# Causal masks of the score maxima: from four 64x128 tile products to four 64x64 tile products

## What is computed

```python
# layer 0
scores = einsum('bhqd,bhkd->bhqk', q, k) / sqrt(8)
causal = triu(ones((s, s), dtype=bool), 1)
scores = where(causal, -inf, scores)
attn_w = softmax(scores, axis=-1)
attn   = einsum('bhqk,bhkd->bhqd', attn_w, v)
```

## Time and profile before

| | |
|---|---|
| three runs | 1511.41, 1514.30, 1517.33 us (median 1514.3) |
| the profiled execution's own time | 1513.78 us |
| its span, first to last instruction | 1512.0 us |
| mean granted clock of PE, of full speed | 0.964 |
| busy share of the span | PE 90%, DVE 83%, ACT 71%, POOL 18% |
| L391 (mask of the maxima) | 1024 matmuls, 68.5 us busy, 222 ns mean |
| layer 0's max units | from 47.2 to 462 us |

### The profile page before, as it was taken

How to read it: one execution, slowest core, us unless ns; L and a number is a source line. 1 busy time by engine, 2 the same in 40 slices (tenths; PEclk the granted TensorE clock), 3 DMA queues, 4 the chain that set the end, 5 groups by cost and what they waited for, 6 DMA issues and landing times.

```text
span 1512.0 us, 31977 instructions
## 1 busy us (share of the span) xinstructions
PE 1366.1 (90%) x13016; PEld 565.2 (37%) x13016; DVE 1251.6 (83%) x1715; ACT 1079.6 (71%) x1239; POOL 278.4 (18%) x624
## 2 busy tenths in 40 slices
PE   6699999999998768888679999999999999999886
PEld 3334434444443235456323332332333333323455
DVE  8988888888884386985899999999999999997043
ACT  6167777777777567763358888888888888888652
POOL 5022313222222151431100000000000000001252
PEclk9689999999999989999889999999999999999998
DMA  5510111101000000021110000000000000000001
GB/s 179 169 44 24 39 31 31 40 24 46 24 4 2 1 1 0 1 81 67 42 64 24 23 24 23 24 21 14 16 23 24 23 23 24 3 3 3 1 15 42
DMA packets 38995, 47.90 MB, mean 32 GB/s; under 512 B 11072, under 2 KB 20160, under 8 KB 38720
## 3 DMA queue, kind: packets, MB, share of 16 engines
q1 hardware_dynamic: 38416, 45.31, 9.8%
q10 hardware_dynamic: 432, 0.53, 0.1%
HBM read 30.22 MB, written 15.47 MB: 30 GB/s over the span
## 4 chain that ended last, share of the span: by engine, by line
PE 73%; DVE 11%; ACT 7%; issue 5%; POOL 3%; DMA 1%; ACTq 0%; POOLq 0%; SPq 0%; DVEq 0%
PE ps L428 29%; PE ps L406 15%; PE ps L385 12%; PE ps L554 7%; DVE l_negp L326 3%; PE ps L445 3%; ACT l_outT L304 2%; ACT shared L298 2%; POOL n_rs L516 2%; PE ps L391 2%; DVE n_bst L497 1%; PE ps L547 1%; PE ps L1042 1%; PE ps L910 1%; PE ps L562 1%
## 5 line engine op out<-in xcount | busy, mean ns | idle before, releaser
L326 DVE TENSOR_REDUCE l_negp<-ps 128x2 f32<-128x1024 f32 (+2 forms) x832 | 956.4, 1181 | 57.7 <-PE ps L391 33.3
L298 ACT ACTIVATE shared<-ps 128x1024 f32<-128x1024 f32 (+1 forms) x832 | 820.5, 991 | 185.3 <-PE ps L406 155.7
L428 PE MATMUL ps<-shared,l_vs 128*32 128x256 f32 (+3 forms) x6648 | 515.4, 385 | 18.9 <-ACT l_outT L304 14.1
L385 PE MATMUL ps<-Ks,Qs 48*128 48x512 bf16 (+3 forms) x1792 | 329.2, 368 | 31.1 <-DVE l_negp L326 22.0
L406 PE MATMUL ps<-Qs,Ks 51*128 51x512 bf16 (+3 forms) x1792 | 321.1, 367 | 14.5 <-ACT shared L298 6.3
L428 PEld LDWEIGHTS ps<-shared,l_vs 128*32 128x32 f32 x6648 | 136.6, 108 | 198.0 <-issue 163.4
L406 PEld LDWEIGHTS ps<-Qs,Ks 51*128 51x128 bf16 x1792 | 81.1, 93 | 316.8 <-issue 181.3
L385 PEld LDWEIGHTS ps<-Ks,Qs 48*128 48x128 bf16 x1792 | 87.5, 94 | 171.8 <-ACT shared L298 96.0
L282 POOL TENSOR_SCALAR_AFFINE_SELECT shared<-shared 128x512 f32<-128x512 f32 x128 | 81.7, 640 | 311.1 <-ACT shared L298 309.0
L267 POOL CAST l_parts<-l_negm 128x16 bf16<-128x16 f32 x64 | 12.6, 197 | 442.3 <-DVE l_negm L331 439.2
L391 PE MATMUL ps<-mask,id 64*128 64x128 bf16 x1024 | 68.5, 222 | 0.0
(11 more groups left out here) (160 smaller groups left out, 1094.7 us busy)
## 6 DMA issues: line engine op xcount, KB each, us to landing
Qs<-scr_q SPq DMA_DIRECT2D x128, 64.0 KB
Ks<-scr_k SPq DMA_DIRECT2D x64, 96.0 KB
Qs<-scr_q SPq DMA_DIRECT2D x128, 32.0 KB
Ks<-scr_k SPq DMA_DIRECT2D x64, 64.0 KB
scr_q<-own SPq DMA_DIRECT2D x4, 768.0 KB, 3.6
scr_q<-shared SPq DMA_DIRECT2D x4, 768.0 KB, 3.5
scr_k<-own SPq DMA_DIRECT2D x4, 768.0 KB, 4.9
scr_k<-shared SPq DMA_DIRECT2D x4, 768.0 KB, 4.8
```

The source lines that it names most:

```text
L298: act.activation(dst, src, ACT.Exp, scale=SCALE).then_inc(exped, 1)
L326: dve.tensor_reduce(dst, src, AX_X, ALU.max, negate=True).then_inc(reduced, 1)
L385: last = pe.matmul(outs[par], Qs[s][r:r + MROW, h2, qt * P:(qt + 1) * P], Ks[s][r:r + MROW, h2, at:at + w], start=True, stop=True)
L428: last = pe.matmul(pv_ps[32 * h:32 * h + 32, a:a + wide], vs[g % 2][:, kt, h, :], pT[m % PRING][:, h, a:a + wide], start=m == u.first_step ...
```

## The change

The four mask matmuls of a group stay four. Half j of the mask now goes only to the output partitions that it can change: j = 0 holds mask rows 0 to 63, which are queries 0 to 63, and j = 1 queries 64 to 127. The output is cut accordingly, so the identity needs 64 columns instead of 128, one copy on each partition half, and it is the same one for both j. For j = 1 the first 64 of the 128 key columns hold no masked entry, so that product has 64 columns instead of 128. The tile of each of these matmuls becomes 64 rows x 64 columns of the array. The set-up has six DMAs instead of eight.

```diff
             if entry[1] == 0:
-                pe.wait_ge(halved, 8 * 16)
+                pe.wait_ge(halved, 6 * 16)
...
                     for j in range(2):
                         for par in range(2):
-                            r = ROWS * par
-                            last = pe.matmul(outs[par][:, w - P:w], id2[r:r + ROWS, j, :], mask2[r:r + ROWS, j, :],
-                                             start=False, stop=True, skip_group_check=True)
+                            r, half = ROWS * par, ROWS * j
+                            last = pe.matmul(outs[par][half:half + ROWS, w - P + half:w], id2[r:r + ROWS, :],
+                                             mask2[r:r + ROWS, j, half:P], start=False, stop=True, skip_group_check=True)
...
-        mask2, id2 = sb("mask2", [P, 2, P], BF16), sb("id2", [P, 2, P], BF16)
+        mask2, id2 = sb("mask2", [P, 2, P], BF16), sb("id2", [P, ROWS], BF16)
...
                 for par in range(2):
+                    rows_of = slice(ROWS * par, ROWS * (par + 1))
+                    sp.dma_start(id2[rows_of, :], ident_bf[0:ROWS, 0:ROWS]).then_inc(halved, 16)
                     for j in range(2):
-                        for to, of in ((mask2, mask_neg), (id2, ident_bf)):
-                            sp.dma_start(to[ROWS * par:ROWS * (par + 1), j, :], of[ROWS * j:ROWS * (j + 1), :])\
-                                .then_inc(halved, 16)
+                        sp.dma_start(mask2[rows_of, j, :], mask_neg[ROWS * j:ROWS * (j + 1), :]).then_inc(halved, 16)
```

## The result

The changed kernel takes 1533.1 us (median of 4 runs, 1528.7 to 1534.2) against 1513.7 us for the kernel before: ratio 1.0112, 95% interval 1.0088 to 1.0135. (The quotient of the two medians is 1.0128; it lies in the interval. In the experiments, too, the ratio is not the quotient with 1513.7: each kernel was timed beside the kernel before, whose median moved between 1513.6 and 1515.9 us.) The forecast was 1531 us. The profiled execution has a span of 1531.5 us.

A forecast was written before the change was run, and what follows sets the result against it. The prediction took PE to bound layer 0's attention from 72.3 to 462 us. Its 9.5 + 8.8 = 18.3 us of PE, 97% on the path, were rounded down to +17: 1513.8 + 17 = 1531 us, range 1508 to 1541.

The forecast's parts named there:

- Which stretch, and who paces it: Layer 0's attention: DVE's maxima pace 47 to 72.3 us, PE paces 72.3 to 462 us.
- Columns taken away, halves side by side: Mask group: column halves of the array work side by side, one 128-column pass, 0.055 us instead of 0.11.
- Going in: From L385's 64x128 tiles to the masks' 64x64 tiles: the shape change costs 0.09 us.
- the first rival: The array does not drain between 64x128 and 64x64: 12.5 us faster, 1501 us; chance 0.15.
- The group and the way out: Mask group L391 to the next product: 0.17 us, whether L428 or L385 follows.
- The sum: Masked groups after 72.3 us: 9.5 + 8.8 = 18.3 us more of PE.
- Both terms: Groups followed by L428: 0.055 us each, 9.5 us; groups followed by L385 or L406: 0.145 us each, 8.8 us.
- The share on the path: After 72.3 us, 97% of mask groups lie on the chain of waits, so +17.7 us of 18.3 counts.
- A free change of shape: No drain between 64x128 and 64x64 at the mask groups: 12.5 us faster, 1501 us; chance 0.15.
- Cost hidden by DVE or ACT: PE is later in the masked part but others set the pace: 1514 to 1519 us; chance 0.13.
- A dearer drain: Each shape change around the masks costs more than 0.09 us, for instance 0.12: 1541 us; chance 0.12.

The follow-up runs named there:

- Experiment 2: The changed kernel with 128 columns for both mask halves, all on 64x64 tiles: 1533.4 us, ratio 1.0103.
- experiment 3: The changed kernel with the masks of both pairs of heads behind both L385 products in units with two groups: 1518.5 us, ratio 1.0012.
- experiment 4: The kernel before with mask half j = 0 on a 64x64 tile and j = 1 on the old 64x128 tile: 1552.7 us, ratio 1.0236.
- experiment 5: The kernel before with the mask as one product per head on the whole 128x128 array: 1540.8 us, ratio 1.0168.
- experiment 7's first kernel: The kernel before with two more zero-adding passes of 64 columns per group on the old tile: 1525.5 us, ratio 1.0081.
- experiment 7: The kernel before plus zero-adding 64-column passes, old tile: two per group 1525.5 us; eight in first groups of two-group units 1524.4; three in last groups 1525.2.
- Experiments 1: The kernel before without its 1024 mask products, maxima of layer 0 taken over unmasked scores: 1495.7 us, ratio 0.9858.
- experiment 6: The kernel before, old 64x128 tile kept: only the second mask half cut to 64 columns, 1512.9 us; both halves cut, 1504.7 us.

## Why the prediction was right

1. *Which stretch, and who paces it*: right. All that moved beyond scatter is the masked stretch; the DVE-bound start took its added PE time for nothing. (The PE lines of the chain add up to 83.5%, not 83.6%; nothing hangs on it.)

2. *Columns taken away, halves side by side*: right, four products in one pass of 128 columns. Experiment 2 shows that the 64 columns contributed 0.007 us a group, and the narrower tile the rest.

3. *Going in*, 0.09 us between 64x128 and 64x64, of which the trace of before had no row: right. 0.32 against 0.22 behind 512 columns. By the medians over all groups it is 0.09 behind 384 and 512 columns, 0.09 to 0.10 behind 256 and 0.10 behind 128. The rule of the Trainium skill, TensorEngine Tiling (Array Packing), Key Properties, that changing the mode drains the engine, agrees with these rows and with experiments 3, 4 and 5. The speedup of narrower tiles, up to 2x, which the Trainium skill gives in TensorEngine Tiling (Array Packing), Theoretical Speedup, is there too: four products in the time of one pass (point 2), 0.055 us instead of 0.11. The changes of shape take more than that gives, and so the first rival, which rested on this gain alone, failed.

4. *The group and the way out*, 0.17 us from the nearest row, L438: right, 0.17.

5. *The sum*: 18.3 us of PE predicted, 20.1 found. Both terms were too small: a first group costs 0.157 us more and not 0.145, and a group ahead of L428 0.06 us more behind 128, 384 and 512 columns and 0.07 behind 256, not 0.055. (My 8.8 and 9.5 us counted 61 and 173 groups; the 9.1 and 11.0 found are of 58 and 176, as the three that L406 follows are last groups.) *The share on the path*: 97% predicted, 86% found. That the two errors cancel, 17.7 and 17.3 us, is luck; with either one alone the forecast of PE's part would have been 15.7 or 19.5 us, still in the range. The 97% were read off the chain of waits as the share of groups that lie on it. I took it that every step of that chain waits for the one before it and for nothing else, so that nothing could be swallowed. That failed: 14% of the change's PE time, and 27% of that of experiment 7's first kernel, did not come through. In the change nearly all of it went into the waits of L385 for ACT (experiment 7), and the share of ACT's exponentials in the chain shrank from 4.1% to 0.2%. Experiments 1, 6 and 7 put the worth of a us of PE here at 0.6 to 0.92 us, by place and size.

6. *The rivals.* A free change of shape: excluded by experiments 3, 4 and 5. Cost hidden by DVE or ACT: partly true, 14% of it. A dearer drain: no, the way in costs 0.09 to 0.10 us behind every width.

## What to carry to other kernels

Before a matmul is cut to a smaller tile, look at its neighbours in the order: a group of products whose tile shape differs from both pays some 0.09 us on each side and for weights that are no longer loaded ahead, more than a 128-column pass (0.055 us) gives back. Cut columns on the tile shape that is already there, or bring products of one shape together (experiment 3: the same products, 13 us less in the masked stretch). Don't read such a change off busy time: that of the masks fell. And don't take a step's share of the chain of waits for the share of a longer step that will come through: here 97% of the groups lay on the chain, and 60 to 92% of the time added or taken away came through, because waits for another engine shrank or grew. A product that only guards a shift which cancels may be worth leaving out: without the masks of the maxima the kernel took 1495.7 us, as long as the unmasked maximum stays near enough to the masked one that the exponentials don't vanish, which depends on the data and was not tried on others.

## What was unexpected

A pass of 64 columns with 128 weight columns costs 0.027 us on the 64x128 tile, half of one with 128 columns: loads of two tiles keep up even then (experiment 6). I had thought a floor near 0.05 us possible.

The weights of a 64x64 group are exposed only because of the change of shape. In experiment 3 the two groups of a unit, eight products, take 0.22 us from the first of them to the weigh step (204.88 to 205.10). One group takes 0.17, so the second adds 0.05, its bare pass, and nothing for its weights.
